# A fused cross-attention and mixture-of-experts kernel: new orders for every engine

## The reference

```python
h     = layernorm(x)
q,k,v = h @ Wq.T + bq, ctx @ Wk.T + bk, ctx @ Wv.T + bv        # 16 heads of 32
p     = softmax(where(mask, clip(q k / sqrt(32), -50, 50), -50))
delta = clip(rs, 0, 0.3) * ((p v) @ Wo.T + bo)
x     = x + layernorm(delta) * gamma + beta
y     = layernorm(x)
gate  = softmax(y @ router.T) * (one of the two largest)
x     = x + sum_e gate_e * (silu(y @ down_e.T) @ up_e)
```

## Time and profile before

| | |
|---|---|
| median of three runs | 189.48 us |
| the profiled execution | 190.05 us, its span 188.3 us |
| TensorE busy | 180.2 us, 96% of the span, 1296 matrix products |
| weight loads | 135.6 us, 72% (beside the products) |
| VectorE busy | 124.5 us, 66% |
| ScalarE busy | 111.2 us, 59% |
| GpSimd busy | 89.2 us, 47% |
| chain that ended last | TensorE 81%, VectorE 6%, DMA 6%, ScalarE 2% |
| mean granted clock of TensorE | 0.999 |

### The profile page before, as it was taken

How to read it: one execution, slowest core, us unless ns; L and a number is a source line. 1 busy time by engine, 2 the same in 40 slices (tenths; PEclk the granted TensorE clock), 3 DMA queues, 4 the chain that set the end, 5 groups by cost and what they waited for, 6 DMA issues and landing times.

```text
span 188.3 us, 3666 instructions
## 1 busy us (share of the span) xinstructions
PE 180.2 (96%) x1296; PEld 135.6 (72%) x1296; DVE 124.5 (66%) x294; ACT 111.2 (59%) x231; POOL 89.2 (47%) x149
## 2 busy tenths in 40 slices
PE   7989999989899999999999999999999999999972
PEld 7966588757274888758688688687786688898951
DVE  2694899989594399231767252673839785778994
ACT  3027608882496955486994217787934795468520
POOL 4032031500869344999596742337384671476200
PEclk9999999999999999999999999999999999999999
DMA  5999976003506300004000330000251000003757
GB/s 150 363 366 325 376 258 176 0 3 98 147 10 234 114 5 0 0 14 115 0 0 3 132 118 3 3 0 0 68 154 34 3 0 0 0 0 115 270 218 295
DMA packets 12210, 19.66 MB, mean 104 GB/s; under 512 B 2336, under 2 KB 4384, under 8 KB 12192
## 3 DMA queue, kind: packets, MB, share of 16 engines
q1 hardware_dynamic: 12192, 19.43, 31.2%
HBM read 14.70 MB, written 4.72 MB: 103 GB/s over the span
## 4 chain that ended last, share of the span: by engine, by line
PE 81%; DVE 6%; DMA 6%; ACT 2%; issue 2%; SPq 2%; ACTq 0%; DVEq 0%
PE ps_r L431 49%; PE ps_v L431 11%; PE ps_t L456 7%; PE ps_v L533 4%; PE ps_v L520 4%; PE ps_r L506 4%; DMA xs<-x 3%; PE ps_r L486 2%; DVE xs L1166 2%; DMA wk<-rz_scratch 2%; ACT stage L758 1%; DMA rz_scratch<-rz 1%; DVE wk L1102 1%; DVE ln_st L1174 1%; SPq L371 1%
## 5 line engine op out<-in xcount | busy, mean ns | idle before, releaser
L431 PE MATMUL ps_r<-hst_hi,wq_hi 128*128 128x512 f32 x64 | 26.6, 415 | 0.2 <-ACT stage L758 0.2
L431 PE MATMUL ps_r<-wo_hi,attt_hi 128*128 128x512 f32 x64 | 26.3, 411 | 0.0
L431 PE MATMUL ps_r<-wo_hi,attt_lo 128*128 128x512 f32 x64 | 25.3, 395 | 0.0
L431 PE MATMUL ps_r<-hst_hi,wq_lo 128*128 128x512 f32 x64 | 25.3, 395 | 0.0
L431 PE MATMUL ps_r<-wo_lo,attt_hi 128*128 128x512 f32 x64 | 25.3, 395 | 0.0
L431 PE MATMUL ps_r<-hst_lo,wq_hi 128*128 128x512 f32 x64 | 25.2, 394 | 0.0
L738 ACT ACTIVATE hs<-xs,ln_bias,ln_rstd 128x512 f32<-128x512 f32 x16 | 12.8, 811 | 18.0 <-POOL ln_bias L1429 18.0
L1441 POOL TENSOR_TENSOR attt_lo<-wk,attt_hi 128x512 fp32r<-128x512 f32 x16 | 20.7, 1312 | 4.1 <-ACT attt_hi L771 4.1
L1437 POOL TENSOR_TENSOR xs<-xs,beta_bc 128x512 f32<-128x512 f32 x16 | 21.0, 1322 | 0.0
L1111 DVE TENSOR_TENSOR cen<-ps_r,gamma_bc 128x512 f32<-128x512 f32 x16 | 10.9, 684 | 13.3 <-ACT cen L816 13.3
L1102 DVE TENSOR_TENSOR wk<-ps_v,wk 128x512 f32<-128x512 f32 x16 | 10.8, 685 | 12.9 <-DMA wk<-rz_scratch 10.4
(11 more groups left out here) (106 smaller groups left out, 399.0 us busy)
## 6 DMA issues: line engine op xcount, KB each, us to landing
wk<-rz_scratch SPq DMA_DIRECT2D x32, 128.0 KB, 2.7
out<-xs SPq DMA_DIRECT2D x16, 256.0 KB, 2.3
xs<-x SPq DMA_DIRECT2D x3, 1024.0 KB, 6.9
wk<-wk_t SPq DMA_DIRECT2D x4, 256.0 KB, 5.4
xs<-x SPq DMA_DIRECT2D x2, 512.0 KB, 6.5
xs<-wv_t SPq DMA_DIRECT2D x1, 1024.0 KB, 9.6
stage<-wq_t SPq DMA_DIRECT2D x1, 1024.0 KB, 11.6
xs<-wo_t SPq DMA_DIRECT2D x1, 1024.0 KB, 12.5
```

The source lines that it names most:

```text
L431: last = pe.matmul(dst, w, m, start=start and i == 0, stop=stop and i == n - 1, skip_group_check=unseen)
```

## The change

It changes no instruction. It writes the lists of all five engines anew, and with TensorE's list the three strings of the rings. All 135 calls of TensorE, 197 of ScalarE, 171 of VectorE, 83 of GpSimd and 44 of SyncE are the same before and after. As it is described, the tensor engine changes less often between long, short and tiled products in the new list. The diff of the rings, of SyncE and of TensorE, and cut parts of the others:

```diff
-    "S31 S32 S33 Q32 Q33 S34 S35 S36 S37 W20 W21 W22 W23 U00 U01 U02 U03 W30 W31 W32 W33 U10 U11 U12 U13 "
+    "S31 S32 S33 Q32 Q33 S34 S35 S36 S37 W20 W21 W22 W23 U00 U01 U02 U03 W30 W31 W32 U10 W33 U11 U12 U13 "
-    "h00 h01 h02 h03 h10 h11 h12 h13 h20 h21 h22 h23 n00 n01 n02 h30 h31 h32 h33 n03 n10 n11 n12 a00 n13 "
-    "a01 n20 n21 a10 n22 a11 n23 n30 n31 a20 n32 a21 n33 a30 a31")
+    "h00 h01 h02 h03 h10 h11 h12 h13 h20 h21 h22 h23 n00 n01 h30 n02 h31 h32 n03 h33 n10 n11 a00 n12 n13 "
+    "a01 n20 n21 a10 n22 n23 a11 n30 n31 n32 a20 n33 a21 a30 a31")
-    "V0 V1 m0 s00 s01 v00 v01 v02 v03 s10 v10 v11 s11 v12 v13 f00 f01 s20 s21 v20 v21 f02 v22 v23 f03 "
-    "f10 s30 f11 s31 f12 v30 v31 f13 v32 v33 f20 f21 f22 f23 f30 f31 f32 f33")
+    "V0 V1 m0 s00 s01 v00 v01 v02 v03 s10 v10 v11 s11 v12 v13 f00 s20 f01 f02 s21 v20 v21 f03 v22 v23 "
+    "f10 s30 f11 s31 f12 v30 v31 v32 v33 f13 f20 f21 f22 f23 f30 f31 f32 f33")
@@ SyncE
             ctx_load(1)
+            wk_load(2)
             wk_load(1)
             x0_load(0)
-            wk_load(2)
             wk_load(3)
...
             small_load()
+            x1_load()
+            wo_load()
+            clean_wait()
+            bv_load()
             gamma_load()
-            x1_load()
-            clean_wait()
-            wo_load()
             bo_load()
             load(2)
-            bv_load()
             experts_load()
...
+            store(1, 1)
+            store(0, 3)
             store(1, 0)
+            store(0, 1)
+            store(0, 2)
+            store(2, 0)
             store(0, 0)
             store(1, 2)
-            store(1, 1)
-            store(0, 2)
+            store(2, 1)
             store(1, 3)
-            store(2, 0)
-            store(0, 3)
-            store(0, 1)
-            store(2, 1)
@@ TensorE
             scores(1, 0)
+            hs_transpose(2, 0)
             weigh(0, 1)
...
             scores(1, 1)
+            hs_transpose(2, 1)
             weigh(1, 0)
-            hs_transpose(2, 0)
-            hs_transpose(2, 1)
+            hs_transpose(2, 2)
             project(0, 0)
             project(0, 1)
-            hs_transpose(2, 2)
+            hs_transpose(2, 3)
             project(0, 2)
-            hs_transpose(2, 3)
             project(0, 3)
             query(2, 0)
-            x1_transpose(0, 0)
             query(2, 1)
             sums(1, 1)
+            x1_transpose(0, 0)
             scores(2, 0)
             weigh(1, 1)
             x1_transpose(0, 1)
             query(2, 2)
+            hs_transpose(3, 0)
             x1_transpose(0, 2)
             query(2, 3)
-            hs_transpose(3, 0)
             down(0, 0)
             scores(2, 1)
+            sums(2, 0)
             down(0, 1)
             hs_transpose(3, 1)
-            hs_transpose(3, 2)
             project(1, 0)
...
             project(3, 2)
+            up(1, 0)
+            x1_transpose(2, 3)
+            hid_transpose(1, 1)
             project(3, 3)
-            x1_transpose(2, 3)
+            down(2, 2)
+            down(2, 3)
             x1_transpose(3, 0)
-            down(2, 2)
-            up(1, 0)
-            down(2, 3)
             x1_transpose(3, 1)
             up(1, 1)
+            x1_transpose(3, 2)
+            down(3, 0)
             hid_transpose(2, 0)
-            down(3, 0)
+            down(3, 1)
             up(1, 2)
             up(1, 3)
-            x1_transpose(3, 2)
-            down(3, 1)
+            x1_transpose(3, 3)
             up(2, 0)
             hid_transpose(2, 1)
-            x1_transpose(3, 3)
-            up(2, 1)
             down(3, 2)
             down(3, 3)
+            up(2, 1)
             hid_transpose(3, 0)
             up(2, 2)
             up(2, 3)
+            hid_transpose(3, 1)
             up(3, 0)
-            hid_transpose(3, 1)
             up(3, 1)
@@ ScalarE, around the last batch's project
             x1_squares(3, 1)
             down_scaled(2, 2)
+            projected_squares(3, 3)
+            down_scaled(2, 3)
             x1_out(3, 0)
-            down_scaled(2, 3)
@@ VectorE: the head, batch 0 to 1, the end
             clean_limited(0)
+            clean_finite(0)
+            clean_marks(2)
             clean_limited(1)
-            clean_finite(0)
+            clean_limited(2)
             clean_finite(1)
-            clean_marks(2)
+            clean_finite(2)
             tile_stats(0, 0)
-            clean_limited(2)
             tile_stats(0, 1)
-            clean_finite(2)
             clean_marks(3)
...
             product(0, 0)
             product(0, 1)
+            centre_wo(3)
             clip(1, 0)
+            clip(1, 1)
             product(0, 2)
-            clip(1, 1)
             product(0, 3)
-            centre_bo()
             reciprocals(1, 0)
+            hs_lo(2, 0)
+            hs_lo(2, 1)
+            scaled(0, 0)
+            product(1, 0)
             tile_stats(3, 0)
...
             residual(3, 2)
             scaled(3, 3)
+            largest(2, 1)
             residual(3, 3)
-            largest(2, 1)
-            finish(1, 0)
             finish(1, 1)
             gating(2, 1)
             hid_lo(2, 0)
+            largest(3, 0)
             finish(1, 2)
             finish(1, 3)
-            finish(2, 0)
-            largest(3, 0)
             gating(3, 0)
             hid_lo(2, 1)
+            finish(2, 0)
+            largest(3, 1)
             finish(2, 1)
-            largest(3, 1)
             hid_lo(3, 0)
             gating(3, 1)
@@ GpSimd, up to batch 1
+            sums_ready()
             ln_power(0, 2)
             ln_power(2, 4)
             batch_power(1)
-            sums_ready()
-            wo_low(0)
             add_beta(0, 0)
             batch_power(2)
+            wo_low(0)
+            wo_low(1)
             add_beta(0, 1)
-            wo_low(1)
+            att_lo(0, 0)
             wo_low(2)
-            wo_low(3)
-            att_lo(0, 0)
             att_lo(0, 1)
             att_lo(0, 2)
+            wo_low(3)
             att_lo(0, 3)
+            residual_powers(0, 0)
+            residual_powers(0, 1)
+            batch_power(3)
+            residual_powers(0, 2)
+            att_lo(1, 0)
+            residual_powers(0, 3)
+            x1_powers(0, 0)
             add_beta(0, 2)
...
```

More of the change, by code:

```diff
@@ L632, in _ @@
             query(2, 2)
+            hs_transpose(3, 0)
             x1_transpose(0, 2)
             query(2, 3)
-            hs_transpose(3, 0)
             down(0, 0)
             scores(2, 1)
+            sums(2, 0)
             down(0, 1)
             hs_transpose(3, 1)
-            hs_transpose(3, 2)
             project(1, 0)
             project(1, 1)
+            hs_transpose(3, 2)
+            project(1, 2)
+            x1_transpose(0, 3)
+            down(0, 2)
             hs_transpose(3, 3)
-            sums(2, 0)
+            project(1, 3)
             sums(2, 1)
-            project(1, 2)
+            x1_transpose(1, 0)
+            query(3, 0)
             weigh(2, 0)
[L648 to L651, removed]
+            x1_transpose(1, 1)
             query(3, 1)
-            x1_transpose(1, 0)
+            down(0, 3)
+            scores(3, 0)
             weigh(2, 1)
-            scores(3, 0)
-            x1_transpose(1, 1)
-            down(0, 3)
+            hid_transpose(0, 0)
             query(3, 2)
+            query(3, 3)
             x1_transpose(1, 2)
-            query(3, 3)
             down(1, 0)
@@ L876, in _ @@
             exp_scores(0, 3)
-            wo_high(1)
             query_out(1, 0)
             query_out(1, 1)
+            hs_norm(2, 0)
+            wo_high(2)
+            exp_scores(1, 0)
             att_hi(0, 0)
-            exp_scores(1, 0)
+            att_hi(0, 1)
+            hs_norm(2, 1)
+            wo_high(3)
             exp_scores(1, 1)
-            wo_high(2)
-            att_hi(0, 1)
+            hs_norm(2, 2)
             att_hi(0, 2)
-            wo_high(3)
             query_out(1, 2)
+            query_out(1, 3)
@@ L888, in _ @@
+            hs_hi(2, 0)
             att_hi(0, 3)
-            hs_norm(2, 0)
-            query_out(1, 3)
-            hs_norm(2, 1)
             exp_scores(1, 2)
             seed(0, 0)
+            hs_hi(2, 1)
+            hs_norm(2, 3)
+            seed(0, 1)
             exp_scores(1, 3)
-            hs_hi(2, 0)
-            hs_hi(2, 1)
-            seed(0, 1)
+            up_high()
+            projected_squares(0, 0)
+            hs_hi(2, 2)
             seed(0, 2)
-            projected_squares(0, 0)
@@ L926, in _ @@
             query_out(2, 3)
+            down_scaled(0, 0)
+            att_hi(1, 3)
             hs_hi(3, 0)
-            att_hi(1, 3)
-            down_scaled(0, 0)
             exp_scores(2, 2)
             seed(1, 0)
+            hs_norm(3, 2)
+            down_scaled(0, 1)
+            hs_hi(3, 1)
+            seed(1, 1)
+            hs_norm(3, 3)
+            exp_scores(2, 3)
```

(41 more changed lines are left out.)

286 lines of the change are left out of this document (129 added, 157 removed).

## The result

| | before | new order |
|---|---|---|
| median of four timed runs each | 189.40 us | 191.78 us, 1.010 times [1.006, 1.014] |
| timed again, 23 and 12 runs (e10 below) | 190.08 us | 191.17 us, 1.0054 times [1.0039, 1.0070] |
| profiled execution, span | 190.05, 188.3 us | 191.41, 189.7 us |

What follows compares the result with a forecast made beforehand. TensorE's own stream was taken as the bound (busy 180.2 of 188.3 us). Terms gave -0.6 up to down(2,3) and +0.4 at the end: -0.2, 189.3 us, no change (chance 0.40), range 188.4 to 190.6.

Steps and rivals of the forecast that it cites:

- Price of a switch: TensorE's stream: entering and leaving tiled calls costs time, long to short is free; +0.52 us, bounds 0 and 0.7.
- Waits that go: TensorE waits at weigh, scores(2,1) and project(1,0) are filled or shortened; -1.41 us, with 0.25 left at scores(2,1).
- Head: Kernel start: x lands later but fewer steps precede clean_finite(3), so keys(3) begins about where it did; -0.1 us.
- Waits that come: Late load(3) delays spread(1,0)'s scratch write and product(1,0); query(2,0) waits +0.45 us, bounds 0 to 1.1; small ones +0.4.
- narrow places: About a dozen TensorE calls left 0 to 0.3 us behind their last producer; +0.4 us, bounds 0 and 1.0.
- the long chain behind load(3): Rival, chance 0.25: late tile_stats(3,3) delays GpSimd up to att_lo(1,3); project(1,0) up to 1 us late; middle 190.1.
- The end: Behind down(2,3): VectorE's run starts 0.32 us later, TensorE's lead becomes idle time; +0.4 us, bounds 0 and 0.7.
- the sign: At hid_transpose(3,1): idle for 1.5 to 2 us ahead of a gating(3,1) that ends near 181.5.
- The rival without new waits: Rival, chance 0.30: load(3) doesn't hold scratch and the tight calls don't wait; 188.7 us.

Runs made afterwards that it cites:

- e10: The new kernel unchanged, timed once more: 1.0054 times the kernel before.
- e8: e1 with sums(2,0) put behind down(0,1) and sums(3,0) behind down(1,1), two more entries into tiled products: 0.9949 times the kernel before.
- e4: The new kernel with the head of the kernel before (wk(2) loaded behind x0, old order of the first steps): 1.0060 times the kernel before, 191.22 us.
- e5: e1 with projected_squares(3,3) ahead of down_scaled(2,2) on ScalarE: 0.9941 times the kernel before, 189.03 us.
- e1: The new kernel with wo_low(3) moved ahead of att_lo(0,1) on GpSimd, so load(3) goes earlier: 0.9950 times the kernel before, 188.94 us.
- e7: The new kernel with load(3) put behind spread(1,0) on SyncE: 0.9992 times the kernel before, 189.79 us.
- e2: The new kernel with add_beta(1,0) and add_beta(1,1) put behind att_lo(1,3) on GpSimd, load(3) still late: 1.0019 times the kernel before, 190.16 us.
- e3: The kernel before with only wo_low(3) moved behind att_lo(0,2) on GpSimd: 1.0137 times the kernel before, median 191.82 us.
- e6: e1 with the three clean steps of clean(3) ahead of tile_stats(0,0) on VectorE: 0.9918 times the kernel before, 188.61 us.

## Why the prediction was wrong

- **Price of a switch: right.** +0.52 forecast; the same prices, summed over the calls as they stand in the trace, give +0.51, and e8 measured two entries by themselves at 0.31. The new order has more dear switches, not fewer, and this is over a third of the loss in the profile.
- **Waits that go: right.** 1.41 forecast; by the table 0.77 went up to project(0,3) and 0.74 behind it, 1.51. My 0.25 left at scores(2,1) wasn't there.
- **Head: wrong by 0.5.** -0.1 forecast; hs_transpose(0,0) came 0.21 later, since x landed at 9.7 and not 9.4, and with 0.16 in batch 0 the stream had lost 0.4 by query(1,0). One profile doesn't settle this term: in the other profiles x landed at 8.9 to 9.9 with this head and at 7.9 to 8.8 with the old one, and e4's runs with the old head were no faster.
- **Waits that come: this step failed.** I put 0.45 on query(2,0) and 0.4 on all narrow places, 0.85 together; 1.97 came, more than the whole loss. I had load(3) at 59.45 and product(1,0) at 69.1; they came at 60.26 and 69.81. So query(2,0) waited 0.76 for 0.45, inside my bounds. And tile_stats(3,3), which I had at about 76.6, ended at 78.09, behind the 77.8 that I had named as the point from which the long chain decides; GpSimd's steps up to att_lo(1,3) took 18.6, where I had 17 to 18.5. So project(1,0) waited 0.92 and x1_transpose(0,2) 0.29. The rival "the long chain behind load(3)", to which I gave 0.25, is what happened, by its own mechanism; its middle, 190.1, was 0.6 above the kernel before where the profiles differ by 1.36: the head's 0.5 and the 0.29 at x1_transpose(0,2) weren't in it. That the landings of this queue come in order, as I wrote, is too strong: in the trace before, three transfers landed 0.2 to 0.7 us ahead of one issued before them. For load(3) and the write behind it, it held in every profile.
- **Why load(3) was 0.8 later than reckoned.** This is read from rows, not tried. wo_low(3) stands behind att_lo(0,2), which waited for att_hi(0,2) and so for product(0,2). That ended at 56.98 and not at 56.2, as clip(1,1) ahead of it started at 55.26, behind exp_scores(1,1), and took 1.12 for its 0.75. VectorE's clip(1,0) and clip(1,1), and GpSimd's att_lo(0,0), wo_low(2) and att_lo(0,1) beside them:

```profile
52.89 1.78 DVE L1092 TENSOR_SCALAR stage<-stage,exp_max 128x1024 f32<-128x1024 f32 x1
55.26 1.12 DVE L1092 TENSOR_SCALAR stage<-stage,exp_max 128x1024 f32<-128x1024 f32 x1 [0.59 <-ACT stage L758]
```

```profile
52.65 1.47 POOL L1441 TENSOR_TENSOR attt_lo<-wk,attt_hi 128x512 fp32r<-128x512 f32 x1
54.08 1.75 POOL L1479 TENSOR_TENSOR wo_lo<-xs,wo_hi 128x512 fp32r<-128x512 f32 x1
55.79 1.75 POOL L1441 TENSOR_TENSOR attt_lo<-wk,attt_hi 128x512 fp32r<-128x512 f32 x1
```

  clip(1,0) started while att_lo(0,0) ran and ended 0.55 us behind it; wo_low(2) ended 1.2 behind clip(1,0), and clip(1,1) 0.55 behind wo_low(2). By these ends they went one after the other, which made some 0.4 of the 0.8; the rest I put down to exp_scores(1,1), which ScalarE now runs behind wo_high(3). A row of the trace before would have warned me: clip(1,1) takes 1.68 there, from 53.55, beside wo_low(2).
- **The end: right in size, half right in reason.** From down(2,3) to up(3,3) it took 0.25 us longer than before, for +0.4; the idle time ahead of hid_transpose(3,1) was 1.5, as foreseen. But e5 shows that the start of VectorE's run wasn't what counted. The last gating ended at 182.98, 1.5 behind the 181.5 that I had set as the sign, as all behind project(1,0) was late.
- **The rival without new waits** (188.7, 0.8 below the kernel before) is near to e1: with load(3) early the new order gains 1.0 us.
- **The whole loss, by the table:** prices +0.51, head +0.39, waits that go -1.51, waits that come +1.97, the stretch up to down(3,3) +0.15, the end -0.15: 1.36 us, as the profiles differ.

## What to carry to other kernels

When a list is written anew, look first at what it does to the transfers: a step that releases a large DMA may have time by its own readers, and still must come well ahead of the next small transfer in the same queue, or that transfer must go first (e1, e7). Filling an engine's waits is worth what was priced here, but a rival that names the point from which it decides deserves more than a quarter when the forecast stands only 1.2 us short of it. Where two engines share long elementwise steps, take their times from rows in which both run.

## What the runs showed of the hardware

- A write of 64 KB issued 0.5 us behind a load of 1 MB in one queue took 4.8 to 5.1 us to land (the new kernel, e2, e3, e4, e10), 2.4 to 2.7 when it was 3 us behind (e1, e5, e6, e8), and 1.5 with nothing ahead (e7). With the load ahead it landed some 0.2 us behind it each time. The Trainium skill, page DMA: Bandwidth & Descriptors, section "Two DMAs through the same engine are not ordered", says that descriptors of one queue of one DMA engine start in order; these landings agree.
- Elementwise steps of VectorE and GpSimd hold each other up: a clip of 0.75 us took up to 1.78, and a GpSimd step of 1.28 took 1.75. The Trainium skill, page SBUF — State Buffer, section "Who interferes with whom", says of VectorE's modes that take the port pair it shares with GpSimd that whichever step issues first has the pair for its whole length, and the other fully blocks. The clip, issued second, ended 0.55 us behind att_lo(0,0), which agrees; no row names the mode that it ran in.
